# Counting edges with interleaved one-hots in narrower spans, and idle transposes in the opening of a graph kernel

## The reference

```python
# x (1024, 512) f32; src, dst (32768,) int32, dst ascending
# layer 0: 0/1 links in both directions plus the diagonal, scaled by degrees
adj = zeros(n, n); adj[src, dst] = 1; adj[dst, src] = 1; adj += eye(n)
h = (adj * dinv[:, None] * dinv[None, :]) @ (x @ W) + b
...
# layers 1 and 3: edges counted with their multiplicity, plus self-loops
out = segment_sum((x @ W)[src] * norm[:, None], dst) + b
...
# layer 2: attention, masked by the links
a = q @ k.T / sqrt(512); a = a * adj + (1 - adj) * NEG
attn = softmax(a) @ v
```

## Time and profile before

| | us |
|---|---|
| median of 3 runs | 585.06 |
| lowest and highest | 584.90, 585.09 |
| the profiled execution | 585.02 |
| its span in the trace | 583.1 |
| what lies around the span | 1.9 |
| PE, DVE, ACT, POOL busy in the span | 564.0, 347.8, 175.8, 126.4 |

### The profile page before, as it was taken

The page is one execution under the profiler, slowest core; times in us unless marked ns, Lnnn a source line. Parts: engine busy times, 40 slices in busy tenths (PEclk is TensorE's granted clock), DMA queues, the critical chain, the costliest instruction groups (busy, mean ns, idle before and its releaser), DMA issues.

```text
span 583.1 us, 6682 instructions
## 1 busy us (share of the span) xinstructions
PE 564.0 (97%) x2145; PEld 349.4 (60%) x2145; DVE 347.8 (60%) x877; ACT 175.8 (30%) x364; POOL 126.4 (22%) x128
## 2 busy tenths in 40 slices
PE   6999999999999999999998999999999999999996
PEld 4555655555788844888864674444444587458743
DVE  7999899948678124335598854665646420450065
ACT  5988689737011221111040000220214202110200
POOL 2000000007432600304162600381600170000011
PEclk9999999999999999999999999999999999999998
DMA  8623000000100000000000000000004000000012
GB/s 300 225 73 144 1 1 1 1 2 1 37 3 0 1 0 0 1 0 1 1 2 1 0 0 1 0 2 0 0 4 159 0 2 0 0 1 0 1 54 92
DMA packets 9431, 16.19 MB, mean 28 GB/s; under 512 B 1572, under 2 KB 1844, under 8 KB 9399
## 3 DMA queue, kind: packets, MB, share of 16 engines
q1 hardware_dynamic: 9398, 15.75, 7.6%
HBM read 13.64 MB, written 2.11 MB: 27 GB/s over the span
## 4 chain that ended last, share of the span: by engine, by line
PE 91%; DVE 5%; ACT 1%; DMA 1%; issue 1%; POOL 0%; SPq 0%; POOLq 0%; DVEq 0%
PE bank L687 15%; PE bank L669 15%; PE bank L739 14%; PE bank L857 10%; PE bank L881 10%; PE bank L598 6%; PE bank L569 5%; PE bank L853 3%; PE bank L577 2%; PE bank L542 2%; PE bank L573 2%; PE bank L869 1%; DMA xs<-in_x_dram 1%; PE bank L530 1%; PE bank L534 1%
## 5 line engine op out<-in xcount | busy, mean ns | idle before, releaser
L454 POOL TENSOR_TENSOR rstd<-veps,mhalf 128x1 f32<-128x1 f32 x32 | 22.8, 711 | 207.6 <-DVE veps L1243 204.7
L1168 DVE TENSOR_SCALAR hot_key<-col_key,keyed 128x320 bf16<-128x320 int16 x256 | 67.1, 312 | 0.0
L881 PE MATMUL bank<-vv,probt 128*128 128x512 f32 x128 | 56.8, 596 | 5.7 <-ACT probt L1077 5.7
L739 PE MATMUL bank<-v_sb,gt 128*128 128x512 f32 (+1 forms) x136 | 55.3, 567 | 0.0
L687 PE MATMUL bank<-adj,y_hi 128*128 128x512 f32 x128 | 51.3, 401 | 0.0
L687 PE MATMUL bank<-adj,y_lo 128*128 128x512 f32 x128 | 50.5, 395 | 0.0
L598 PEld LDWEIGHTS bank<-hot_key,hot_lo 128*128 128x128 bf16 x256 | 25.1, 98 | 38.8 <-DVE hot_key L1168 16.8
L1250 DVE SCALAR_TENSOR_TENSOR xs<-bank,dinv,xs 128x512 f32<-128x512 f32 x23 | 17.0, 749 | 49.7 <-PE bank L739 37.2
L598 PE MATMUL bank<-hot_key,hot_lo 128*128 128x320 bf16 x256 | 45.4, 300 | 0.0
L881 PEld LDWEIGHTS bank<-vv,probt 128*128 128x128 f32 x128 | 23.9, 190 | 35.1 <-issue 27.7
L964 ACT ACTIVATE apart<-col_lo,edge_key 128x128 bf16<-128x128 int16 x128 | 43.8, 391 | 0.0
(11 more groups left out here) (216 smaller groups left out, 1035.2 us busy)
## 6 DMA issues: line engine op xcount, KB each, us to landing
w_sb<-in_L_gnn_W_dram SPq DMA_DIRECT2D x3, 1024.0 KB, 5.6
xs<-in_x_dram SPq DMA_DIRECT2D x2, 1024.0 KB, 7.4
v_sb<-in_L_gnn_W_dram SPq DMA_DIRECT2D x2, 1024.0 KB, 7.3
out_dram<-xs SPq DMA_DIRECT2D x7, 256.0 KB, 2.0
w_sb<-in_L_gnn_weight_dram SPq DMA_DIRECT2D x4, 256.0 KB, 6.2
wq_sb<-in_L_gnn_Wq_dram SPq DMA_DIRECT2D x1, 1024.0 KB, 10.9
wk_sb<-in_L_gnn_Wk_dram SPq DMA_DIRECT2D x1, 1024.0 KB, 13.5
wv_sb<-in_L_gnn_Wv_dram SPq DMA_DIRECT2D x1, 1024.0 KB, 7.7
```

The source lines that it names most:

```text
L739: mm = pe.matmul(bank[:, 0 if cols is high_cols else HALF * (s % 2) + b, cols], g(k, j), w[:, k, cols], start=k == 0, stop=k == FB - 1)
L881: mm = pe.matmul(bank[:, 6 + m % 2, :], probt[:, m % 2, j, :], vv[:, j, :], start=j == 0, stop=j == NB - 1)
L1168: V.tensor_scalar(hot_key[:, slot * CPG + c, :], col_key[:], keyed[:, 0, bass.ds(g + c * G, 1)], None, ALU.is_equal).then_inc(hot_set, 1)
```

## The change

- The window shrinks from 40 to 24 nodes and is kept for two chunks (PAIR = 2, 256 edges) instead of four: a group has SPANS = 2 spans with a place of their own. KEYS is 192. A group's four products go to two halves of a bank, and two additions of 192 elements take them to `count`.
- DVE's one-hots for two chunks are made by one comparison of two tensors, with the two chunks interleaved element by element: `lo_near` [128, 128, 2] and `hot_key` [128, 192, 2]. The edges' values are read as pairs, again and again (`to_broadcast`), from new int16 tables `lo16` and `key16`. PE reads every second element.
- The two additions are set apart: the one of the first span, then `lo_near` of group g + 3, then the one of the second span, then the two `hot_key`.
- DVE's loop has 16 groups a turn (BODY); two register loads of four places each stand at every fourth group.
- ACT computes its distances one group ahead, in three buffers.
- Transposes stand in pairs between the four products of an `xw` unit. EARLY grows to 28 pieces, which hold eight transposes of x's second half; SHARE is 1280 and a transpose is weighed with 200 instead of 128.
- PE gets 34 transposes of the identity at the opening, which nobody reads (`idle_turns`). POOL's part of the zeroing of `count` waits for `rows_set`.
- Behind the counting, four of DVE's `low` steps come one block earlier.

```diff
-WIN = 40
+WIN = 24
+PAIR = 2
 BY_DVE = 2
-EARLY = 24 * 128
-SHARE = 1300
+EARLY = 24 * 200 + 4 * 1024
+SHARE = 1280
+TURNED = 200
...
-BODY = 8
+BODY = 16
...
+            elif kind == "xw":
+                for m, first in ((n - 1, 0), (n + 1, 2)):
+                    ORDER += [(n, first), (m, 0), (m, 1), (n, first + 1), (m, 2), (m, 3)]
...
+            pool.wait_ge(rows_set, 2)
             nc.gpsimd.memset(count[:, ZEROED:NB, :].bitcast(F32), 0.0).then_inc(const_set, 1)
...
+            def idle_turns(count_):
+
+                for n in range(count_):
+                    pe.transpose(bank[:, HALF + 3, 0:P], ident[:], ident[:])
+
             pe.wait_ge(const_set, 1)
+            idle_turns(16)
             for n in range(3):
                 if n < 2:
                     pe.wait_ge(act_rows_set, n + 1)
                 else:
+                    idle_turns(6)
                     pe.wait_ge(rows_set, 1)
...
+            idle_turns(8)
             pe.wait_ge(rows_set, 2)
...
+            def chunk(slot, c):
+                span = slice(c // PAIR * KEYS, (c // PAIR + 1) * KEYS)
+                lo = lo_near[:, slot, :, c] if c < BY_DVE else lo_far[:, slot, c - BY_DVE, :]
+                return pe.matmul(bank[:, slot, span], lo, hot_key[:, slot, c // PAIR, :, c % PAIR],
+                                 start=c % PAIR == 0, stop=c % PAIR == PAIR - 1)
...
             for g in range(G):
+                if 0 < g < G - 1:
+                    if g >= 2:
+                        act.wait_ge(act_hot_set, g - 1)
+                    distances(g + 1, (g + 1) % 3)
                 if g >= SLOTS:
                     act.wait_ge(win_summed, g - SLOTS + 1)
-                low_one_hots(g, g % SLOTS, g)
+                far_one_hots(g % SLOTS, g % 3, g)
...
+            def low_one_hots(g, slot):
+
+                V.tensor_tensor(lo_near[:, slot], col_near[:],
+                                lo16[:, bass.ds(g, 1), :].to_broadcast([P, P, BY_DVE]), ALU.is_equal)
+
+            def key_one_hots(g, slot):
+
+                for n in range(SPANS):
+                    V.tensor_tensor(hot_key[:, slot, n], col_key[:],
+                                    key16[:, bass.ds(g, 1), n * PAIR:(n + 1) * PAIR].to_broadcast([P, KEYS, PAIR]),
+                                    ALU.is_equal).then_inc(hot_set, 1)
...
+            def one_group(g, at_dst, seen, slot, ahead):
 
                 dve.wait_ge(win_summed, seen + 1)
                 dve.wait_ge(win_added, seen + 2)
...
+                add_span(at_dst[0], slot, 0).then_inc(span_added, 1)
+                if ahead is not None:
+                    low_one_hots(ahead, (slot + AHEAD) % SLOTS)
+                dve.wait_ge(span_added, seen + 1)
+                add_span(at_dst[1], slot, 1).then_inc(win_added, 1)
+                if ahead is not None:
+                    key_one_hots(ahead, (slot + AHEAD) % SLOTS)
...
                     for n in range(BODY):
-                        one_hots(q * BODY + (n + AHEAD), (n + AHEAD) % SLOTS)
-                        add_window(places[n], r * G + q * BODY + n, n % SLOTS)
...
+                        if n % HALF == 0:
+                            places = places_at(q * BODY + n)
+                        one_group(q * BODY + n, places[n % HALF], r * G + q * BODY + n, n % SLOTS, q * BODY + (n + AHEAD))
...
-                if 3 <= h < 3 + HALF:
-                    low(h - 3, ya, xw[:, h - 3, :], dinv[:, 0, h - 3:h - 2])
+                if 2 <= h < 2 + HALF:
+                    low(h - 2, ya, xw[:, h - 2, :], dinv[:, 0, h - 2:h - 1])
```

## The result

The changed kernel takes **578.02 us** (median of 5 runs, 577.68 to 578.85 and one of 580.93) against 585.09: ratio 0.989, 95% interval 0.9867 to 0.9914, 7.1 us less. The forecast was 579.2. The profiled execution took 577.68 us, span 575.8. PE is still busy for 96% of it (rows 1 had 97%).

A forecast was written before the change was run, and what follows sets the result against it. PE was taken to bound the counting stage, DVE nearly a second bound. From 585.02 us, -13.6 (one-hot products) + 4.3 (DVE becoming slower) + 3.5 (opening) gave 579.2 us, range 571.5 to 589.

The forecast's parts named there:

- two terms that the sum had at 0: Counting stage: waits for ACT, and PE's other pieces with transposes paired between products, were each taken to cost nothing.
- PE's products: Counting stage: one-hot products shrink from 320 to 192 columns, 0.54 to 0.32 us a group, 13.6 us less.
- DVE's group: Counting stage: at two elements a cycle, DVE needs 1.28 us a group instead of 1.57, before register loads.
- The loads: DVE's register loads every fourth group: 1.5 us a pair, 0.96 uncovered, bringing DVE to 1.52 us a group.
- the 4.3 of the sum: Counting stage: DVE slower than PE by 6.6 us, 3.2 of it free, 0.9 added by long groups: 4.3 us more.
- The risk: Register loads dear, at 2.3 us for two: DVE takes 1.72 us a group, total 591.2 us; chance 0.13.
- The opening: Before the first group: 34 idle transposes don't raise PE's clock and only take time, 3.5 us more.
- early-clock rival: Opening: idle transposes raise the clock early, +0.1 us instead of +3.5, total 575.8 us with the same loads; chance 0.20.
- Pairing and ACT: Counting stage: pairing transposes between products costs PE 0; ACT, with 17 us free in 100, also 0.
- wrong if PE waits for ACT's copies: Stated sign against the forecast: PE waiting for ACT's copies, which it had costed at 0.
- The end of the stage: Behind the counting: the seven link rows start near 119 us instead of 123.27.

The follow-up runs named there:

- experiment 5: Changed kernel with the key one-hots of a pair of chunks laid out one behind the other instead of interleaved: 591.78 us.
- experiment 9: Spans of 20 instead of 24 targets, on the kernel with whole units, TURNED 128, 22 idle transposes, one load of eight and SHARE 1224: 569.08 us.
- Experiment 4: Changed kernel with the second addition right behind the first and the low one-hots behind both: 584.31 us.
- experiment 3: Register loads of the changed kernel: doubled (not in what ran) 578.24 us; one of eight 577.33; every second group, pairs of two 592.09, of four 600.28.
- experiments 2: Changed kernel with its units whole again, no transposes in pairs between the products of x with w0: 575.35 us.
- experiment 6: Changed kernel with whole units, and a transpose counted as 128 instead of 200 (TURNED and EARLY): 576.53 us.
- experiment 7: Kernel of experiment 6 with 22 instead of 34 idle transposes: 575.47 us.
- 8: Kernel of experiment 7 with one register load of eight places instead of two of four, and SHARE 1224 instead of 1280: 571.8 us.
- second measurement of the changed kernel: Meant to make each register load twice, but the second loads were not in the kernel that ran, so the changed kernel measured again: 578.24 us.
- experiment 1: Changed kernel without its 34 idle transposes in the opening: 579.2 us.

## Why the prediction was right, point by point

The time was met to 1.2 us, and that is luck: its steps were partly wrong and cancelled. Against -13.6 + 4.3 + 3.5 stand -12.6 for the products, +1.25 of waiting for DVE, -0.5 in the opening, and two terms that the sum had at 0: +3.4 of waiting for ACT and +1.1 for the other pieces.

**PE's products**: forecast 0.32 us a group, measured 0.346, so -12.6 instead of -13.6 us. Scaling by columns was right: without the 4-byte step four products do take 0.33 us (experiment 5). The step itself costs the rest, about 0.015 us a group, which the sum took as free. With it the price is 0.0865 us at 192 columns and 0.072 at 160 (experiment 9), 0.45 ns a column in both, near the 0.44 of the fp32r products that the prediction had beside it.

**DVE's group**: forecast 1.28 us, measured 1.30. Two elements at a time in both comparisons (forecast 0.20 and 0.27, measured 0.23 and 0.27), additions 0.27, the second 0.50 behind the first. Experiment 5 shows that the rate hangs on the interleaving. The Trainium skill (Vector Engine (DVE) Microarchitecture Reference, section 5.1) says so for an operation with two sources: a row read again and again keeps two elements at a time, one element read again and again does not. The traces agree, with 0.27 against 0.47 us. Experiment 4 shows what the additions would have cost.

**The loads**: a term of the right kind and the wrong size. Forecast 1.5 us a pair and 0.96 uncovered; in this kernel it is 1.13 from the comparisons' start and 0.59 uncovered. So DVE takes 1.45 us a group on average, not 1.52, and PE, without its waits, takes 1.45 too, not 1.41: DVE did not become the slower one, and PE waits 1.25 us for it instead of the 4.3 of the sum. The price of 0.75 a load was taken from idle times that hold a branch; a load of four places here takes 0.34 us by itself, and the trace of before had one of eight at 0.60 (experiment 3). The risk was real: with loads of two places, or of four begun at the wrong place, the same pair leaves 0.97 or more uncovered.

**The opening**: the step that failed. I took transposes for work that doesn't raise the clock, from the row that 8.01 to 11.48 brought no rise. In the changed kernel the clock rose at 4.9 us, behind nothing but idle transposes. In experiments 2, 6, 7 and 8, and in the second measurement of the changed kernel, the distances fall between 6.5 and 7.5 us, behind idle transposes and turns of key rows, and x's transposes run at 0.11 us. The Trainium skill (TensorE: Matmul & The Clock Gate, part 4) says that transposes don't count as busy in the same way; for these fp32 transposes the runs here contradict that. Why x's own sixteen, before and in experiment 1, brought no rise while they ran is open. Forecast +3.5, measured -0.5. The early-clock rival had this right: x's transposes at 9.5, product through at 12.1, wait for x until 13.0 (forecast 13.64). In the second measurement, with x at 14.05, the same count gives +0.6.

**Pairing and ACT**: costed at 0, with "wrong if PE waits for ACT's copies" beside it. It does, 3.4 us from start to start in two places, and 2.7 us come back without the pairs. I had counted how much work ACT has, not when: the last copy of a matrix stands behind the next group's distances, and the pairs had moved the product away that used to cover it.

**The end of the stage**: the link rows were forecast near 119 and came at 114.57, since DVE didn't fall behind; the time didn't follow, because PE was the bound to its first turn.

## What to carry to other kernels

- Work added to bring the clock up early pays only until PE needs something else, here the upper half of x. Trim it to what the rows show.
- When a filler schedule is tightened, look at the stage behind it: work that it takes from there leaves waits, and a waiting TensorE can lose its clock as well.
- A result that the next product needs wants another product in between, however idle the engine that copies it is on average.
- Before an instruction is priced from the idle time around it, look whether the trace times the instruction itself.

## What the runs showed of the hardware that was not expected

- Idle transposes alone bring TensorE from 1.2 to 2.4 GHz: they start 0.213 us apart from 2.02 us on and 0.109 apart from 4.97. When it happens differs: in the second measurement of the same kernel it was 7.2 us.
- Short waits can cost the clock. In experiment 7, waits of 0.43, 1.18 and 1.19 us with 0.6 us of transposes between were followed by a granted clock of 0.61 over 4 us; that cost about 1.6 us (the eight products 1.19, the turn of a link row 0.42). In experiment 5's trace, waits of 0.71 and 0.76 us that ended at 47.5 and 49.2 were followed by 0.61 from 50 to 54 us. In experiment 6's trace the same three waits as in 7, and in the changed kernel one of 1.50 and one of 1.67, were not.
- A register load on DVE from a table in SBUF: 0.34 us for four places that begin at a multiple of four, 0.60 for eight, 0.53 for two, and 0.97 for four that begin two places further. It runs beside comparisons queued ahead, which covered 0.54 us of a pair in the changed kernel and 0.94 in experiment 5.
- A moving operand of bf16 that steps over every second element: 0.345 us for four products of 192 columns, 0.33 without the step.
